# LSTM and mixture layer on one core: how many columns each recurrent product moves, unread products after it, and the recurrent state kept in halves

## What is computed

```python
xW = jnp.einsum('ntd,dk->tnk', x, Wx) + b
def step(carry, xw_t):                       # 1024 times, one after another
    prev_h, prev_c = carry
    a = xw_t + prev_h @ Wh                   # (2, 256) @ (256, 1024)
    i, f, o = sigmoid(a[:, :H]), sigmoid(a[:, H:2*H]), sigmoid(a[:, 2*H:3*H])
    g = tanh(a[:, 3*H:])
    next_c = f * prev_c + i * g
    next_h = o * tanh(next_c)
x = x + hs
# then, for every token: two shared experts (silu), a router over 8 experts, top 2 of 8 experts (gelu)
x = x + (shared_out + routed_out) / 4
```

## Time and profile before

| | |
|---|---|
| median of 3 runs | 2022.76 us (2022.18 to 2022.83) |
| the profiled execution | 2023.38 us |
| its span, first to last instruction | 2021.6 us |
| busy: PE, PEld, DVE, ACT, POOL | 82%, 72%, 80%, 40%, 7% |
| mean granted TensorE clock | 0.997 of full speed |

### The profile page before, as it was taken

One profiled execution on the slowest core, in us unless ns is written; L12 is line 12 of the kernel. 1 busy time (PEld: TensorE's weight loads), 2 busy tenths in 40 slices (PEclk: granted clock), 3 DMA queues, 4 the chain that ended last, 5 costly groups with the idle time before them and its releaser, 6 DMA issues. The chain is left out here.

```text
span 2021.6 us, 95636 instructions
## 1 busy us (share of the span) xinstructions
PE 1655.5 (82%) x37356; PEld 1456.2 (72%) x37356; DVE 1619.1 (80%) x14263; ACT 806.0 (40%) x5529; POOL 135.1 (7%) x457
## 2 busy tenths in 40 slices
PE   7888888788888888888888887888888888888888
PEld 6777777777777777777777776777777777777777
DVE  6888788787878878788787877878788787887874
ACT  3554343343433434343343433434334343433432
POOL 0000000000000000000000000000000000000000
PEclk9999999999999999999999999999999999999999
DMA  5000000000000000000000000000000000000000
GB/s 232 3 3 3 3 6 3 6 3 3 6 3 6 3 3 6 3 6 3 6 3 3 6 3 6 3 3 6 3 5 3 4 4 3 6 3 6 3 3 7
DMA packets 7223, 19.85 MB, mean 10 GB/s; under 512 B 1136, under 2 KB 5616, under 8 KB 5872
## 3 DMA queue, kind: packets, MB, share of 16 engines
q1 hardware_dynamic: 6768, 13.73, 1.8%
HBM read 11.63 MB, written 2.10 MB: 7 GB/s over the span
## 5 line engine op out<-in xcount | busy, mean ns | idle before, releaser
L687 PE MATMUL gates<-hh,wh_lo 128*128 128x32 f16 x16384 | 820.7, 194 | 349.1 <-DVE hh L608 346.1
L687 PEld LDWEIGHTS gates<-hh,wh_lo 128*128 128x128 f16 x16384 | 597.9, 98 | 544.5 <-DVE hh L608 541.2
L695 PE MATMUL gates<-hh,wh_hi 128*128 128x32 f16 x16384 | 696.7, 183 | 4.2 <-DVE hh L620 4.2
L578 DVE TENSOR_TENSOR_SCAN gates<-part_fac,gates 128x12 f32<-128x12 f32 x3072 | 395.6, 186 | 262.3 <-PE gates L695 238.7
L330 ACT ACTIVATE gates<-gates 128x4 f32<-128x4 f32 x1024 | 161.8, 158 | 1051.5 <-DVE gates L578 1051.5
L695 PEld LDWEIGHTS gates<-hh,wh_hi 128*128 128x128 f16 x16384 | 572.9, 96 | 6.1 <-DVE hh L620 6.1
L340 ACT ACTIVATE to<-o_sum 128x4 f32<-128x4 f32 x1024 | 212.3, 207 | 116.0 <-DVE o_sum L578 0.8
L605 DVE TENSOR_SCALAR to<-to 128x4 f32<-128x4 f32 x1024 | 175.0, 171 | 71.3
L597 DVE TENSOR_TENSOR_SCAN gates<-gates,addend 128x12 f32<-128x12 f32 x1024 | 194.9, 190 | 0.0
L591 DVE SCALAR_TENSOR_TENSOR addend<-gates,c_now 128x4 f32<-128x4 f32 x1024 | 167.7, 164 | 25.1
L333 ACT ACTIVATE addend<-gates 128x8 f32<-128x8 f32 x1024 | 182.2, 178 | 0.0
(11 more groups left out here) (131 smaller groups left out, 1571.3 us busy)
## 6 DMA issues: line engine op xcount, KB each, us to landing
rw_sb<-rw SPq DMA_DIRECT2D x2, 2048.0 KB, 22.2
sw_sb<-sw SPq DMA_DIRECT2D x3, 1024.0 KB, 13.3
outT<-osb SPq DMA_DIRECT2D x16, 128.0 KB, 2.2
x_sb<-xT SPq DMA_DIRECT2D x1, 1920.0 KB, 9.7
wh_sb<-wh SPq DMA_DIRECT2D x1, 1024.0 KB, 4.7
wx_sb<-wx SPq DMA_DIRECT2D x1, 1024.0 KB, 6.5
x_sb<-xT SPq DMA_DIRECT2D x1, 128.0 KB, 4.8
eye_sb<-eye SPq DMA_DIRECT2D x1, 64.0 KB, 6.0
```

What stands on the lines that cost most here:

```text
L578: return v.tensor_tensor_scan(dst, part_fac[:].rearrange("p c j -> p (c j)"), parts[q], 0.0, ALU.mult, ALU.add)
L687: mm(copies(q, m, n)[:, :, :, 0:1], wh_lo[:, c, (q * KC + m) * P:(q * KC + m + 1) * P], again(hh[:, c, :, 1:2], n), start=(m == 0 and c == ...
L695: last = mm(copies(q, m, n)[:, :, :, 0:2], wh_hi[:, c, (q * KC + m) * P:(q * KC + m + 1) * P], again(hh[:, c, :, :], n), start=False, stop ...
```

## The change

1. `low` repeats its columns 12 times (24 columns); `high` repeats 7 times for G and O (28 columns) and not at all for F and I (4 columns).
2. After the piece of each step `fill` issues four matmuls of 128 fp16 columns into a part of the `acc_lg` bank that nobody reads; not in steps 1, 2, 62 and 63 of tiles 1 to 15.
3. `hh` holds the two halves of h apart, so that `low` reads neighbours and `high` reads in steps of two.
4. Scratch columns move from 256 to 384 of a bank (`BESIDE`), and `o_sum` moves from SBUF to the bank of F.
5. DVE seeds G and I before `h_hi`, F behind h, and O last; `h_lo` comes before `c_now`. PE multiplies `low` G, I, F in this order, and waits for the seeds of F and of O (`s_seeded`).
6. The split of x leaves POOL: ACT makes `x_hi` in step 60, DVE `x_lo` in steps 61 and 63.

```diff
-WIDE = 32
+LOW_COPIES, HIGH_COPIES = 12, 7
+FILL = 4
+BESIDE = 384
-SPLIT_AT = 5
+SPLIT_HI, SPLIT_LO = 60, (61, 63)
-        hh = sb("hh", [P, KC, B, 2], F16)
+        hh = sb("hh", [P, KC, 2, B], F16)
@@ POOL: split() and its calls go
@@ ACT
+            def split_hi(tile):
+                activation(x_part[0][:], x_sb[:, :, (tile + 2) * TT:(tile + 3) * TT], ACT.Identity, scale=s_xin).then_inc(s_parts, 1)
@@ DVE, lstm
-                v.tensor_copy(gif_xw, of_gif(seeds[:, piece % 2, at, 0:O * HC]))
+                v.tensor_copy(gi_xw, of_gi(seeds[:, piece % 2, at, 0:F * HC]))
...
                 v.tensor_tensor(h_now, to1[:], tc, ALU.mult).then_inc(s_own, 1)
+                v.tensor_copy(f_xw, seeds[:, piece % 2, at, F * HC:O * HC]).then_inc(s_seeded, 1)
+                dve.wait_ge(s_own, 2 * s + 2)
+                v.scalar_tensor_tensor(h_lo, h_hi, -LO, by_batch(h_now), ALU.mult, ALU.add).then_inc(s_hlo, 1)
                 ins = v.tensor_scalar(c_now[:], cs[:, :, 2], 0.5, None, ALU.mult)
...
-                v.tensor_copy(o_xw, seeds[:, piece % 2, at, O * HC:GATES])
-                dve.wait_ge(s_own, 2 * s + 2)
-                v.scalar_tensor_tensor(h_lo, h_hi, -LO, by_batch(h_now), ALU.mult, ALU.add).then_inc(s_hlo, 1)
+                v.tensor_copy(o_xw, seeds[:, piece % 2, at, O * HC:GATES]).then_inc(s_seeded, 1)
+            def split_lo(k, tile):
+                dve.wait_ge(s_parts, tile + 1)
+                ins = v.scalar_tensor_tensor(x_part[1][:, k, :], x_sb[:, k, (tile + 2) * TT:(tile + 3) * TT], s_xin,
+                                             x_part[0][:, k, :], ALU.mult, ALU.subtract)
@@ PE
+            def fill():
+                for j in range(FILL):
+                    mm(acc_lg[:, BESIDE:BANK], wh_hi[:, 0, j * P:(j + 1) * P], wh_hi[:, 1, 0:BANK - BESIDE], start=False, stop=True,
+                       skip_group_check=True)
...
+            def lstm(s, tile):
                 pe.wait_ge(s_hhi, s + 1)
-                low(F)
                 low(G)
                 low(I)
+                if s:
+                    pe.wait_ge(s_seeded, 2 * s - 1)
+                elif tile:
+                    pe.wait_ge(s_seeded, 2 * TS - 1)
+                low(F)
                 pe.wait_ge(s_hlo, s + 1)
-                high(F).then_inc(s_mul, 1)
-                high(G).then_inc(s_mul, 1)
-                high(I).then_inc(s_mul, 1)
+                high(F, 1).then_inc(s_mul, 1)
+                high(G, HIGH_COPIES).then_inc(s_mul, 1)
+                high(I, 1).then_inc(s_mul, 1)
+                if s:
+                    pe.wait_ge(s_seeded, 2 * s)
+                elif tile:
+                    take_back(pe, s_seeded, 2 * TS)
                 low(O)
-                high(O).then_inc(s_mul, 1)
+                high(O, HIGH_COPIES).then_inc(s_mul, 1)
```

More of the change, by code:

```diff
@@ L156, in cond_resid_kernel @@
         hw0 = sb("hw0", [P, GATES])
-        hh = sb("hh", [P, KC, B, 2], F16)
-        h_lo, h_hi = hh[:, :, :, 0], hh[:, :, :, 1]
+        hh = sb("hh", [P, KC, 2, B], F16)
+        h_lo, h_hi = hh[:, :, 0, :], hh[:, :, 1, :]
         h32 = sb("h32", [P, 2, HS, HC])
@@ L260, in _ @@
             stage(0, slice(GATES, (HS + 1) * GATES))
[L262 to L269, removed]
             def piece(q, tile):
@@ L339, in lstm @@
                 act.wait_ge(s_sum, 5 * s + O_OF)
-                activation(to[:], last_of(o_sum[:]), ACT.Tanh, scale=0.5).then_inc(s_tanh, 1)
+                activation(to[:], last_of(o_sum), ACT.Tanh, scale=0.5).then_inc(s_tanh, 1)
                 act.wait_ge(s_sum, 5 * s + C_OF)
@@ L379, in _ @@
                 first_tile(s)
+                if s == SPLIT_HI:
+                    split_hi(0)
             take_back(act, s_sum, 5 * TS)
@@ L386, in _ @@
                     mixture(s, xw_at)
+                    if s == SPLIT_HI and it < NT - 1:
+                        split_hi(it)
                 take_back(act, s_sum, 5 * TS)
@@ L397, in _, with of_gi @@
             done = [0]
-            def of_gif(columns):
+            def of_gi(columns):
                 return columns.rearrange("p (q c) -> p q c", c=HC)
@@ L592, in lstm @@
                 dve.wait_ge(s_mul, 4 * s + O_OF)
-                summed(o_sum[:], O).then_inc(s_sum, 1)
+                summed(o_sum, O).then_inc(s_sum, 1)
                 dve.wait_ge(s_scan, 3 * s + 3)
@@ L657, in _ @@
                 first_tile(s)
+                if s in SPLIT_LO:
+                    split_lo(SPLIT_LO.index(s), 0)
             round_end()
@@ L663, in _ @@
                     mixture(s, ch)
+                    if s in SPLIT_LO and it < NT - 1:
+                        split_lo(SPLIT_LO.index(s), it)
                 round_end()
@@ L676, in copies, with high @@
                 return at[:, :, m * B * PARTS:(m + 1) * B * PARTS].rearrange("p r (b j) -> p r b j", j=PARTS)
-            def again(at, n):
-                return at.rearrange("p b (r j) -> p r b j", r=1).broadcast_to([P, n, B, at.shape[2]])
             def low(q):
-                n = WIDE // B
+                n = LOW_COPIES
                 for m in range(KC):
                     for c in range(KC):
[L687 to L692, removed]
+                        mm(copies(q, m, n)[:, :, :, 0], wh_lo[:, c, (q * KC + m) * P:(q * KC + m + 1) * P],
+                           hh[:, c, 1:2, :].broadcast_to([P, n, B]), start=(m == 0 and c == 0), stop=False, skip_group_check=True)
+            def high(q, n):
                 for m in range(KC):
                     for c in range(KC):
-                        last = mm(copies(q, m, n)[:, :, :, 0:2], wh_hi[:, c, (q * KC + m) * P:(q * KC + m + 1) * P],
-                                  again(hh[:, c, :, :], n), start=False, stop=True, skip_group_check=True)
-                return last
+                        last = mm(copies(q, m, n)[:, :, :, 0:2],
+                                  wh_hi[:, c, (q * KC + m) * P:(q * KC + m + 1) * P],
+                                  hh[:, c, :, :].rearrange("p (r j) b -> p r b j", r=1).broadcast_to([P, n, B, 2]),
+                                  start=False, stop=True, skip_group_check=True)
+                return last
+            def fill():
+                for j in range(FILL):
+                    mm(acc_lg[:, BESIDE:BANK], wh_hi[:, 0, j * P:(j + 1) * P], wh_hi[:, 1, 0:BANK - BESIDE], start=False, stop=True,
+                       skip_group_check=True)
             def product(ps, w, at):
@@ L836, in _ @@
                 first_tile(s)
+                fill()
             take_back(pe, s_hhi, TS)
@@ L844, in _ @@
                 for s in range(TS):
-                    lstm(s)
+                    lstm(s, it)
                     mixture(s, True)
+                    if s not in (LOGITS, LOGITS + 1, LAST, LAST + 1):
+                        fill()
                 take_back(pe, s_hhi, TS)
```

30 lines of the change are left out of this document (13 added, 17 removed).

## The result

The changed kernel takes **1959.64 us** (median of 4 runs, 1959.03 to 1960.02), the kernel before on the same chip 2022.47 (2022.13 to 2022.83): ratio 0.9689, 95% interval 0.9672 to 0.9706. It is faster by 62.8 us.

The account below looks back on a forecast made before the run. One chain around three engines, a step's length 1023 times, was taken as the bound. From 2023.4: -59.3 (58 ns a step) - 7.6 + 1.1 + 11.9 + 8 = 1977.5, so 1977 us; 8 in 10 range 1960 to 2000.

Parts of the forecast that it names:

- Fewer columns in `low`: PE's twelve `low` ahead of `high` F: slots go from 29 to 25 ns, 0.35 becomes 0.30, 50 ns a step.
- 28 columns in G and O: PE's `high` of G reads in steps of two, so its four slots cost 3 ns a step.
- Four columns in `high` F and I: Last matmul to the F and I sums: 28 columns fewer at 0.375 ns each, 11 ns; slots taken as staying 25.
- short slots: Rival: 4-column slots on PE take 16 ns, I sum 60 to 72 ns earlier still, 1903 to 1915 us; chance 0.05.
- The split off POOL: Steps 48 and 49, lengthened by POOL's split of x, become plain: 0.48 a tile, 16 tiles, -7.6 us.
- The halves of h in time: `h_lo` starts at 0.28, fits by 0.05; seed waits free in plain steps, +1.1 us for O's seed at step 0.
- Unread products: Four fp16 products take 0.22 in PE's 0.43 of empty queue before the next `low`: covered, no cost.
- What DVE gives back: DVE's extra copy and `h_lo` wait make F sums late in full steps: 0.79 a tile, 15 tiles, +11.9 us.
- everything of the mixture is 0.10 later: DVE's mixture instructions behind h start 0.10 later, the first at 0.49 where L545 started at 0.39.
- half of it, if the slots close up: Lower bound on the 11.9 us that DVE's later work was to cost; the upper bound was twice.
- The clock: PE's clock falls at 8 of 15 tile ends, 1.0 us each: +8 us, bounds 0 and 15 to 30.
- The rival of falls everywhere in the tile: Rival: too few columns, clock down in many steps; at a third of the steps about 2120 us; chance 0.04.

Follow-up runs that it names:

- run 3: The changed kernel with 32 columns in `low` and in `high` of G and O, halves of h still apart: 2001.08 us, plain step 1.887.
- run 2: The changed kernel with `high` of F and I at 28 columns again, like G and O: 1964.95 us, plain step 1.850.
- run 11: run 5 with 8 columns in `low` and 4 in `high` of every gate: 2022.97 us, clock 0.903.
- Run 1: The kernel before with only the split of x moved from POOL to ACT and DVE: 2016.63 us, ratio 0.9965.
- run 7: The changed kernel with DVE's old order, `o_sum` in SBUF again and no waits for seeds: 1975.63 us, plain step 1.850.
- run 12: run 5 with twelve unread products a step in place of four: 2116.89 us, plain step 2.002.
- run 5: The changed kernel with unread products in every step, also in steps 1, 2, 62 and 63: 1952.28 us, ratio to before 0.9646.
- run 4: The changed kernel without the four unread products of each step: 1959.81 us, clock 0.982.
- run 10: run 5 with the copy of F's seeds moved from DVE to ACT and `c_now` ahead of `h_lo`: 1945.72 us, ratio to before 0.9619.
- run 9: The changed kernel with unread products in steps 62, 63, 0, 1 and 2 alone: 1951.49 us, ratio to before 0.9645.

## Why the prediction was right and where it was wrong

The mechanism was right: fewer columns on the way from `h_hi` to the I sum, the split, and something given back through DVE and the clock. What failed are the sizes of two terms, the plain step (58 ns, measured 69) and what DVE gives back (11.9 + 1.1 us, measured 6.8). The terms one after another; as measured they add up to 63.4 us, against 63.2 from first to last `h_hi`:

- **"Fewer columns in `low`", 50 ns, and "28 columns in G and O", -3 ns.** The last `high` of I starts 806 ns after `h_hi`, before 858: 52 less where 47 were forecast. `low` took 314 ns to the first `high` instead of 359, the `high` of F, G and I together 275 instead of 280, and the first `low` starts 2 ns sooner. The 3 ns for G's reading in steps of two do not exist (run 3 shows `high` with 32 such columns at 25). Right in kind, 5 ns too small.
- **"Four columns in `high` F and I", 11 ns.** The matmul that ends ahead of the I sum takes 165 ns, before 182 to 183: 17. The slope from 128 to 32 columns, 0.375 ns each, does not go on down to 4, it is steeper there, 0.6 ns each (17 over 28 columns); run 2 measures the same thing as 16 ns a step. The 72 ns for short slots never came, as the forecast had it: slots stand at 25 ns down to 4 columns, in run 11 too. Together with the point above: 69 ns a step, not 58, and 1023 steps make the **11 us** that are most of the miss.
- **"The split off POOL", -7.6.** Run 1 has -6.6 with 4 to 10 us open, and steps 48 and 49 are plain.
- **"The halves of h in time".** `h_lo` at 0.28 and no wait, as forecast; run 7 shows what it would have cost without the new order and `o_sum`'s new place together, 16 ns a step.
- **"Unread products"** are covered, as forecast, and run 12 shows where the cover ends, by its own sum.
- **"What DVE gives back", +11.9 and +1.1.** Measured over 15 tiles, as medians over the plain step: step 5 +102 ns, 14 +78, 15 +75, 20 +62, 0 +40, 63 +32, 11 +30, 8 +20, 17 +11: 0.45 a tile, **6.8 us**. The forecast had 0.15 for step 5's F sum, 0.15 and 0.06 around steps 14 and 15, and 0.33 for steps 63 and 0, which are 0.07. The step that failed is "everything of the mixture is 0.10 later". It holds for L545, 0.39 after `h_hi` before and 0.49 now, but the first of the small instructions stood at 0.42 and moved to 0.49, 0.07 later; and they then follow each other at 0.07 where they stood at 0.08. In step 5 the F sum moved 0.056, from 0.890 to 0.946. The `take_back`s on DVE in step 63 did not come on top. The bound "half of it, if the slots close up" was near, and for that reason.
- **"The clock", +8 for 8 falls of 1.0 us.** There were 10 in the loop, at tile ends, and run 5 prices them at 7.4 us together. Right in sum, and the place too. But no run shows a term of 8 falls at 1.0 us: the kernel before has one fall at the 15 tile ends of the loop, 0.90 us over two plain steps, and the change has ten, 0.74 us each by run 5's price. That the estimate came so near is in part luck. The mean clock of 0.984 is a little under the 0.99 that the forecast had named as a sign of being wrong; it comes from these falls. The rival of falls everywhere in the tile did not come, not even without the unread products (run 4), but run 11 shows that this rival was no fancy: with fewer columns still, it costs 71 us over run 5. No idle time of PE over 0.90 us stands ahead of any of the ten, and between two runs the falls go with columns: the change and run 2 have the same matmuls at the same slots and differ in columns alone, with ten falls and one, and the same longest idle time of 0.90.

Sum: -70.6 (1023 x 69 ns), -7.6, +6.8, about +8: -63.4. The forecast's errors were 11 us in the plain step and 6 us in DVE's part, both on the cautious side, so they added up rather than cancelled, and 1960 as the lower end was 0.4 us too high. Half of DVE's part and no falls together would have given 1963 by the forecast's own sum, so it was the plain step that needed bounds: it had none but the short slots, although no row had a product with so few columns.

## What to carry to other kernels

Where one chain through three engines sets the step, count each slot and each drain on it, then ask what each engine does behind the chain: here DVE's part cost 7 us, and with the extra copy on ACT, busy 41% of the span, about half of that came back (run 10), though step 8 got longer where POOL then starts earlier. Here, useless work for the clock's sake paid only where PE is sparse: run 9 has it in 5 of 64 steps and gains 8 us over the change, which has it in 60 and gains nothing from it (run 4). Trim the last product ahead of a waited sum (16 ns a step in run 2), but look at the sparse places for what the clock then loses.

## What was not expected of the hardware

- A matmul of 4 columns takes 165 ns and one of 28 takes 180 to 181, one of 32 takes 182 to 183, with slots of 25 ns for all of them; 32 columns written as single elements stand at 29 ns and 24 so written at 25 (runs 2, 3, 11).
- The clock answers to columns that are only repeated: with 24 and 28 of them in `low` and in `high` of G and O it stays up inside a tile (0.997 and 0.996 in runs 5 and 9), with 8 and 4 it is down for long stretches (0.903 in run 11), though PE has as many matmuls and four products of 128 columns in every step.
- Two DVE instructions of 128x8 took 0.23 and 0.21 us instead of 0.16 where POOL's `h_part` and `x_new` ran beside them (run 10, step 8, against run 5).
- The tanh of O takes 173 ns from PSUM into SBUF and 207 from SBUF into SBUF; that of F takes 158 within PSUM.
- The three sums, which DVE takes at 0.10 apart when PE delivers them so, follow at 0.04 and 0.08 when F is late (946, 990, 1066 ns in step 5).
